# Routing tokens to experts: selection-matrix products on TensorE replaced by indirect DMAs through memory

## What is computed

```python
cap = max(1, int(T * CAP_FACTOR / E))          # 512 * 1.25 / 8 = 80
probs_full = jax.nn.softmax(xt @ gate_w, axis=-1)
top_p, top_i = lax.top_k(probs_full, K)        # K = 2 of E = 8
for k in range(K):
    e, w = top_i[:, k], top_p[:, k]
    pos = ...                                  # how many earlier tokens chose e in choice k
    keep = pos < cap
    buf = zeros((E, cap, D)).at[e, pos_c].set(xt * keep, mode='drop')
    h = gelu(einsum('ecd,edf->ecf', buf, w1) + b1)             # 512 -> 2048
    y = einsum('ecf,efd->ecd', h, w2) + b2                     # 2048 -> 512
    y = y + einsum('ecr,erd->ecd', gelu(einsum('ecd,edr->ecr', buf, wd)), wu)
    out = out + y[e, pos] * keep * w
sh = gelu(xt @ sw1 + sb1) @ sw2 + sb2 + gelu(xt @ swd) @ swu   # a shared expert for all tokens
out = out + 0.2 * sh
```

## Time and profile before

| | us |
|---|---|
| median of 3 runs (2127.96 to 2133.68) | 2129.24 |
| the profiled execution | 2133.98 |
| its span in the trace | 2132.3 |
| of it, from the first expert's first product to the last one's end | 1758.4 to 2117.3 |
| PE busy | 2012.3 (94%) |
| DVE / ACT / POOL busy | 1193.0 / 1038.2 / 292.6 |

### The profile page before, as it was taken

How to read it: one execution, slowest core, us unless ns; L and a number is a source line. 1 busy time by engine, 2 the same in 40 slices (tenths; PEclk the granted TensorE clock), 3 DMA queues, 4 the chain that set the end, 5 groups by cost and what they waited for, 6 DMA issues and landing times. The chain is left out here.

```text
span 2132.3 us, 33366 instructions
## 1 busy us (share of the span) xinstructions
PE 2012.3 (94%) x10596; PEld 1662.8 (78%) x10596; DVE 1193.0 (56%) x2660; ACT 1038.2 (49%) x2357; POOL 292.6 (14%) x234
## 2 busy tenths in 40 slices
PE   7899999999999999999999999998797999999998
PEld 6787777877877778777877887786653789999997
DVE  3456666667666655666766766665766430222113
ACT  3202766676676661066676676668254431111111
POOL 0200112211211122011211112122232000000000
PEclk9899999999999999999999999999899999999998
DMA  7452111111111245311111111113003325544440
GB/s 217 165 175 82 36 42 42 45 32 47 42 33 37 61 157 180 121 33 38 53 30 44 40 34 47 35 43 91 30 0 101 148 113 220 198 191 160 160 161 20
DMA packets 121890, 186.66 MB, mean 88 GB/s; under 512 B 11896, under 2 KB 69424, under 8 KB 117712
## 3 DMA queue, kind: packets, MB, share of 16 engines
q1 hardware_dynamic: 119136, 181.06, 25.4%
q10 hardware_dynamic: 2672, 4.55, 0.7%
HBM read 146.78 MB, written 38.80 MB: 87 GB/s over the span
## 5 line engine op out<-in xcount | busy, mean ns | idle before, releaser
L698 DVE TENSOR_TENSOR crs_ptl<-crs_tp,crs_pth 128x512 fp32r<-128x512 f32 x512 | 352.2, 690 | 226.7 <-ACT crs_pth L566 225.7
L566 ACT ACTIVATE crs_pth<-crs_tp 128x512 fp32r<-128x512 f32 x512 | 305.1, 596 | 209.8 <-PE crs_tp L910 209.8
L495 POOL TENSOR_TENSOR crs_vl<-crs_vraw,crs_vh 128x512 fp32r<-128x512 f32 x128 | 165.1, 1290 | 1117.3 <-ACT crs_vh L573 1117.3
L901 PE MATMUL crs_ring<-crs_kh,crs_ql 128*128 128x512 f32 x512 | 235.2, 459 | 3.9 <-DVE crs_ql L738 3.9
L920 PE MATMUL crs_ov<-crs_ptl,crs_vh 128*128 128x512 f32 x512 | 208.6, 407 | 19.0 <-DVE crs_ptl L698 19.0
L910 PE MATMUL crs_tp<-all_ident,crs_prob 128*128 128x128 f32 x1024 | 197.3, 274 | 26.7 <-ACT crs_more L560 26.7
L910 PEld LDWEIGHTS crs_tp<-all_ident,crs_prob 128*128 128x128 f32 x1024 | 138.6, 140 | 101.7 <-ACT crs_more L560 44.3
L901 PE MATMUL crs_ring<-crs_kh,crs_qh 128*128 128x512 f32 x512 | 202.8, 396 | 0.0
L920 PE MATMUL crs_ov<-crs_pth,crs_vh 128*128 128x512 f32 x512 | 202.3, 395 | 0.0
L901 PE MATMUL crs_ring<-crs_kl,crs_qh 128*128 128x512 f32 x512 | 201.8, 394 | 0.0
L920 PE MATMUL crs_ov<-crs_pth,crs_vl 128*128 128x512 f32 x512 | 200.2, 391 | 0.0
(11 more groups left out here) (264 smaller groups left out, 3594.2 us busy)
## 6 DMA issues: line engine op xcount, KB each, us to landing
moe_w<-in_L_ffn_w SPq DMA_DIRECT2D x48, 1024.0 KB, 11.6
v_scratch<-crs_more SPq DMA_DIRECT2D x64, 512.0 KB, 2.9
crs_vraw<-v_scratch SPq DMA_DIRECT2D x128, 256.0 KB, 2.7
ex_w<-in_L_ffn_w SPq DMA_DIRECT2D x16, 1024.0 KB, 12.0
crs_prob<-in_ctx SPq DMA_DIRECT2D x32, 256.0 KB, 3.9
crs_wo<-in_L_xattn_Wo SPq DMA_DIRECT2D x16, 512.0 KB, 4.1
moe_w<-in_L_ffn_sw SPq DMA_DIRECT2D x8, 1024.0 KB, 14.3
qry_wq<-in_L_xattn_Wq SPq DMA_DIRECT2D x16, 256.0 KB, 4.3
```

The source lines that it names most:

```text
L495: nc.gpsimd.tensor_tensor(vl[:, n % VR, :, :], vraw[:, :, :], vh[:, n % VR, :, :].bitcast(F32), ALU.subtract).then_inc(s["v_lo"], 1)
L566: act.activation(pth[:, k % PT, :], tp[k % PT][:, :], ACT.Copy).then_inc(s["pt_hi"], 1)
L698: v.tensor_tensor(ptl[:, k % PT, :], tp[k % PT][:, :], pth[:, k % PT, :].bitcast(F32), ALU.subtract).then_inc(s["pt_lo"], 1)
L901: m = pe.matmul(ring[at % RING][:, :], a[:, t // RT, rows], w[:, n % KR, :], start=i == 0, stop=i == 2)
```

## The change

Two buffers in the device memory are added: `buf_dram` (8 experts x 2 choices x 80 slots x 512 words) and `y_dram` (the same for seven experts).

**Tokens to experts.** At the start of `experts` POOL clears `xe`, and SP writes these zeros over `buf_dram` in four DMAs. DVE works out for each token and choice the row in `buf_dram` (`idx`; a token that has no place gets a row past the end). POOL then writes the token rows there with eight indirect DMAs of 128 rows (2 KB a row). For every expert SP loads its 160 rows into `xe` (`rows_load`), PE turns them with 16 transposes (`fetch`) and ACT puts them into `bufT`. `fetch(e + 1)` stands in each expert but the last between its two layers. `gather`, `sel`, `xh` and `xl` are gone.

**Outputs back.** The turned rows of experts 0 to 6 go as they are to `y_rows` (ACT, no split), and SP writes them to `y_dram` (`rows_store`). When expert 6's have landed, POOL fetches for every token and choice its row with eight indirect DMAs into `y_got` (in the buffer of expert 6's `w1`, cleared by POOL first), and DVE adds these 8 tiles to `X` (`residual_got`) during expert 7. Only expert 7 still goes through `comb` and `scatter`.

The core of the diff:

```diff
         def _(sp):
+            sp.wait_ge(s["consts"], 1)
+            for m in range(E // 2):
+                sp.dma_start(buf_dram[2 * m:2 * m + 2, :, :, :].rearrange("e k s d -> s (e k) d"), xe[:, :, :, :].rearrange("s q k d -> s (q k) d")).then_inc(s["zeroed"], 16)
             expert_loads(0, 0)
-            sp.wait_ge(s["x_hi"], 2)
+            sp.wait_ge(s["routed"], TT * K * 16)
+            rows_load(0, 0)
             sp.wait_ge(s["sh_ps"], FC)
             expert_loads2(0, 0)
+            sp.wait_ge(s["xe_ld"], 16)
+            rows_load(1, 1)
...
                     sp.wait_ge(s["y_ps"], e * 2 + 2)
                     expert_loads(e + 2, q)
                     expert_loads2(e + 2, q)
+                    rows_load(e + 2, q)
+                    rows_store(e, q)
+            rows_store(E - 2, 0)
...
         def _(pool):
+            nc.gpsimd.memset(xe[:, :, :, :], 0.0).then_inc(c, 1)
...
+            pool.wait_ge(s["zeroed"], E // 2 * 16)
+            pool.wait_ge(s["ids_ok"], K)
+            for i in range(TT):
+                for k in range(K):
+                    nc.gpsimd.indirect_dma_start(buf_dram[:, :, :, :].rearrange("e k s d -> (e k s) d"), bass.IndirectOffsetOnAxis(idx[:, i, k:k + 1], 0),
+                                                 xn[:, i, :], None, bounds_check=E * SL - 1, oob_is_err=False).then_inc(s["routed"], 16)
+            pool.wait_ge(s["y_ps"], (E - 2) * 2 + 2)
+            nc.gpsimd.memset(y_got, 0.0).then_inc(c, 1)
+            pool.wait_ge(s["y_st"], E * 16)
+            for i in range(TT):
+                for k in range(K):
+                    nc.gpsimd.indirect_dma_start(y_got[:, i, k, :], None, y_dram[:, :, :, :].rearrange("e k s d -> (e k s) d"),
+                                                 bass.IndirectOffsetOnAxis(idx[:, i, k:k + 1], 0), bounds_check=(E - 1) * SL - 1, oob_is_err=False).then_inc(s["routed"], 16)
...
         def _(v):
+            def residual_got():
+                v.wait_ge(s["routed"], 2 * TT * K * 16)
+                for k in range(K):
+                    for i in range(TT):
+                        v.scalar_tensor_tensor(X[:, i, :], y_got[:, i, k, :], topp[:, i, k:k + 1], X[:, i, :], ALU.mult, ALU.add).then_inc(s["chain"], 1)
...
+            biased(0)
+            with v.Fori(1, E - 1) as e:
                 biased(e)
+            residual_got()
+            combine(E - 1)
+            biased(E - 1)
             turned(E - 1)
-            residual(E - 1)
+            residual()
...
         def _(pe):
+            def fetch(e, j, early=False):
+                pe.wait_ge(s["xe_ld"], e * 16 + 16)
+                if not early:
+                    pe.wait_ge(s["yt_hi"], e * K - K)
+                for m in range(2):
+                    for c in range(2):
+                        for k in range(K):
+                            at = c * SL + k * CAP
+                            p = pe.transpose(t_ps[m][:, at:at + CAP], xe[:, j, k, (2 * m + c) * P:(2 * m + c + 1) * P], ident[0:CAP, 0:CAP])
+                    p.then_inc(s["g_ps"], 1)
...
                 for n in range(3):
                     layer1(5 + n)
-                    if not first:
-                        pe.wait_ge(s["r_ok"], e + 1)
-                        scatter(e - 1, before == 1, 2 * n, 2 * n + 2)
-                if pair is not None:
-                    gather(pair + 1)
+                if not last:
+                    fetch(e + 1, 1 - i, first)
```

More of the change, by code:

```diff
@@ L1352, in _, with experts @@
                 m.then_inc(s["out_ps"], 1)
-def experts(nc, a, out, X, ident):
+def experts(nc, a, out, buf_dram, y_dram, X, ident):
     E, K = 8, 2
@@ L1377, in experts @@
     LOWEST = -87.5
+    NOWHERE = 65536.0
     with ExitStack() as ctx:
@@ L1723, in hidden, with turned, expert @@
                 m.then_inc(s["h_ok"], 1)
-            def turned(e):
+            def turned(e, q):
+                act.wait_ge(s["y_st"], e * 16)
                 for k in range(K):
                     act.wait_ge(s["yt_ps"], e * K + (k + 1))
-                    act.activation(yh[:, k, :], t_ps[k][0:CAP, :], ACT.Copy).then_inc(s["yt_hi"], 1)
-            def expert(e, first, pair=None):
+                    act.activation(y_rows[:, q, k, :], t_ps[k][0:CAP, :], ACT.Copy).then_inc(s["yt_hi"], 1)
+            def expert(e, q, first=False, last=False):
                 for n in range(4):
@@ L1851, in turn, with scatter @@
                     m.then_inc(s["yt_ps"], 1)
-            def scatter(e, first, start, stop):
-                if start == 0:
-                    pe.wait_ge(s["comb_ok"], e + 1)
-                    pe.wait_ge(s["yt_lo"], e * K + K)
-                for n in range(start, stop):
+            def scatter():
+                pe.wait_ge(s["yt_lo"], 2 * K)
+                for n in range(K * TT):
                     k, i = n // TT, n % TT
-                    if not (first and n < 2):
-                        pe.wait_ge(s["c_ok"], e * (K * TT) + (n - 1))
+                    if n >= 2:
+                        pe.wait_ge(s["c_ok"], n - 1)
                     for part in (yl, yh):
@@ L1863, in scatter, with expert @@
                     m.then_inc(s["c_ps"], 1)
-            def expert(e, i, uses, before, pair=None):
-                first = before == 0
+            def expert(e, i, uses, first=False, last=False):
                 pe.wait_ge(w1_ld[i], uses * 64)
-                pe.wait_ge(s["g_ok"], uses * KC)
+                pe.wait_ge(s["g_ok"], e * 2 + 2)
                 def layer1(n):
@@ L1911, in expert @@
                         m.then_inc(s["y_ps"], 1)
-                    if c == 0 and not first:
-                        scatter(e - 1, before == 1, 6, K * TT)
-            pe.wait_ge(s["x_hi"], 2)
             pe.wait_ge(s["rows_ok"], K)
             pe.wait_ge(s["so_ok"], 2)
-            gather(0)
+            fetch(0, 0, True)
             pe.wait_ge(s["so_ok"], TT)
             pe.wait_ge(s["sh_ok"], FC)
-            expert(0, 0, 1, 0)
-            expert(1, 1, 1, 1, 0)
-            with pe.Fori(0, (E - 4) // 2) as m:
-                expert(m * 2 + 2, 0, m + 2, 2)
-                expert(m * 2 + 3, 1, m + 2, 2, m + 1)
-            expert(E - 2, 0, E // 2, 2)
-            expert(E - 1, 1, E // 2, 2)
+            expert(0, 0, 1, first=True)
+            expert(1, 1, 1)
+            with pe.Fori(1, (E - 2) // 2) as m:
+                expert(m * 2, 0, m + 1)
+                expert(m * 2 + 1, 1, m + 1)
+            expert(E - 2, 0, E // 2)
+            expert(E - 1, 1, E // 2, last=True)
             turn(E - 1)
-            scatter(E - 1, False, 0, K * TT)
+            scatter()
 def perceiver(nc, a, out):
@@ L1947, in perceiver @@
             selfattn(nc, a, X, ident, prob)
-        experts(nc, a, out, X, ident)
+        experts(nc, a, out, buf_dram, y_dram, X, ident)
 def kernel(**inputs):
```

114 lines of the change are left out of this document (48 added, 66 removed).

## The result

| | before | after |
|---|---|---|
| median (us) | 2131.46 (2127.96 to 2133.73, 4 runs) | 2146.43 (2143.38 to 2147.17, 4 runs) |
| the profiled execution / its span | 2133.98 / 2132.3 | 2143.38 / 2141.6 |

The account below looks back on a forecast made before the run. PE's own instructions were taken to bound the kernel. +17.1 (experts 1 to 6) + 0.9 - 3.1 - 3.5 = +11.4 us gave an expected median of 2140.6 us, own range 2131 to 2149, overall range 2122 to 2155.

Parts of the forecast that it names:

- The wait: Experts 1 to 6: PE stands still 5.7 us before the fetch, for rows queued behind 8.5 MB of weights.
- the landing: SP's queue: the rows are there 25.3 us after the expert's start; bounds on average 24.6 and 26.3.
- The fetch: PE, between an expert's two layers: sixteen transposes per fetch, taken as 1.75 us.
- The clock: PE after each wait: granted clock falls to 0.50, costing 1.7 us on average; bounds 0 and 2.3.
- The price per expert: Experts 1 to 6: 25.3 + 1.75 + 20.0 + 1.7 = 48.75 us each, +17.1 in all.
- The front: Before expert 0: the gather becomes 16 transposes, most at 1.2 GHz, and a wait for ACT's copy; -3.5 us.
- The tail: Expert 7: eight indirect fetches take about 7.8 us back to back, within 19.7 us of room; cost 0.
- the third rival: Expert 7: POOL's fetches come one after another and make DVE 5.9 us late; 2146.5 us, chance 0.15.
- Rival 1: Experts 1 to 6: rows land at 24.6 us and the clock holds; 2126.2 us, chance 0.17.
- Rival 2: Experts 1 to 6: no wait, rows do not stand behind the weights; -33.0 us, 2096.2 us, chance 0.08.
- Expert 0: Expert 0: no wait; PE's gap of 0.86 us before the second layer is filled by 1.75 of transposes; +0.9 us.
- Expert 7: Expert 7: loses 3.74 us of scatter and gets back 0.6 of the gap between its layers; -3.1 us.

Follow-up runs that it names:

- filled wait: Changed kernel with 24 more products, results unused, on PE between first layer and fetch in experts 1 to 6: 2135.67 us.
- both halves: Outputs back by indirect DMAs alone: 2109.69 us; routing by DMA alone, rows ahead of weights, against the kernel before: 2115.95 us.
- one moved line: Changed kernel with SP issuing the load of an expert's rows ahead of that expert's weights instead of behind them: 2096.35 us.

## Why the prediction was right

**The wait** (the main term) was right in its place and its cause: six waits ahead of the fetch of experts 2 to 7, 6.7 us each where 5.7 were predicted. The mis-sized term is the landing: PE's first transpose came 26.6 us after the expert's start on average in place of 25.3, outside the bounds of 24.6 to 26.3. (The terms written down for it, 23.7 + 0.8 + 0.6, give 25.1, not 25.3.) It was the weights ahead of the rows and not the rows. In the trace of the changed kernel the last 1 MB of `w2` landed 24.5 to 26.4 us after the expert's start, 25.7 on average (in the expert shown issued at 1849.99 and there 15.6 us later); in the kernel before, whose times I had carried over, 23.6 to 25.5, on average 24.5. The rows landed 0.8 behind the weights, and PE began 0.1 later. Why the weights came 1.2 us later in this trace than in that one is not shown. The 358 GB/s of the Trainium skill's page "DMA: Bandwidth & Descriptors" (Specifications), by which the wait would have been 7.9 us, do not explain it: the queue moved 383 to 391 GB/s in this trace in the eight us up to 1863, and what the wait had more than predicted came behind that.

**The fetch** was miscounted: eight transposes, not sixteen. The row of the turn, eight in 0.87 us, was read rightly and doubled wrongly. The fetch cost 0.6 us at full clock (1815.39 to 1816.00 above), not 1.75, and 1.1 at the half clock; half of the bound by the 80 columns, 0.55, comes near it.

**The clock** fell as predicted. I took 1.7 us with bounds up to 2.3. In the rows of the changed kernel it cost 2.2: 0.5 more in the fetch and 1.7 on average in the first group of the second layer (5.67 to 7.04 in place of 4.61). The filled wait measured 1.8 to 2.1.

**The price per expert** came out at 26.6 + 0.6 + 20.0 + 2.2 = 49.4 (49.46 measured) against the predicted 48.75: the landing 1.3 and the clock 0.5 too low, the fetch 1.15 too high. That these errors nearly cancel is luck. With eight transposes in 0.87 the six experts would have been predicted 5.3 us lower, and the front and expert 0 together some 2, so that by the same working the sum would have been near +4. The wait and the half clock are the right mechanism; that the number came so close is not their merit alone.

**The front** gave back 5.7 in place of 3.5: the fetch to expert 0's first product took 1.44 us. PE had not stopped ahead of it, so the transposes ran at full clock, and they are eight:

```profile
1746.23 0.77 PE L1883 MATMUL moe_bank<-all_ident,moe_xe 80*128 80x80 f32 x8
1746.76 0.77 ACT L1749 ACTIVATE moe_bufT<-moe_bank 128x320 f32<-128x320 f32 x2 [8.14 <-PE moe_bank L1883]
...
1747.67 2.74 PE L1914 MATMUL moe_bank<-moe_bufT,moe_w 128*128 128x160 f32 x9 [0.67 <-ACT moe_bufT L1749]
```

**The tail** is hidden, as forecast, and the third rival did not come. From the timeline of expert 7 of the changed kernel, which began at 2085.80 (L1545 the indirect fetches, L1660 `residual_got`, L1667 the bias of the expert's output):

```profile
2100.07 1.06 POOL L1545 DMA_INDIRECT moe_w<-y_scratch,moe_idx  x1 [10.62 <-DMA y_scratch<-ex_y_rows]
...
2109.28 1.00 POOL L1545 DMA_INDIRECT moe_w<-y_scratch,moe_idx  x1 [0.30 <-issue]
2112.70 5.51 DVE L1660 SCALAR_TENSOR_TENSOR all_X<-moe_w,moe_topp,all_X 128x512 f32<-128x512 f32 x8 [26.00 <-DMA moe_w<-y_scratch,moe_idx]
2118.25 0.88 DVE L1624 TENSOR_SCALAR ex_comb<-moe_rows,moe_ecol 80x512 fp32r<-80x512 f32 x2
...
2126.76 0.68 DVE L1667 TENSOR_SCALAR ex_yT<-moe_bank,moe_b_cols 128x160 f32<-128x160 f32 x2 [7.06 <-PE moe_bank L1938]
```

POOL fetches from 14.3 us into the expert (13.8 predicted), the eight take 12.6 us together (7.8 taken, bound 25.6), and DVE has 7.06 us to spare. The formula of the same page (Anatomy of one DMA) for one DMA from POOL, which the prediction put eight times in a row for an estimate of 20.8, is not what came: they go out 1.30 us apart, and the last is there 3.4 us after it began.

**Rival 1** (a cheaper wait) did not come: no rows landed before 25.5 us and the clock fell each time. **Rival 2** (no wait) was false for this kernel, and its price was near: 33.0 us less than before was worked out for rows that do not stand behind the weights, and with them ahead it is 35.8 (the experts take 40.85 us in place of 41.35, by the cheaper fetch).

**The rest.** Expert 0's +1.45 (0.9 predicted) is not the transposes, which only fill its gap of 0.86 in part. In the changed kernel the clock is 0.50 from about 1747.2 to 1750.7, at the start of expert 0, and its first 40 products take 12.56 us in place of 11.11: the half clock that stood in front of expert 0 before (1752 to 1755.2) has moved into it. So this term came near for another reason than the one given. Expert 7's -2.7 (-3.1 predicted) is the scatter's 3.74 less a gap of 0.92 before its second layer, which stays open.

## What to carry to other kernels

A small load that an engine waits for, issued behind megabytes on one queue, arrives when the megabytes have; issue it ahead of them or on another queue, and look at the whole queue before believing that traffic is free. A wait in an in-order engine costs what is queued behind it, and on PE the idle time is charged a second time by the clock (here 6.7 us of wait and about 2 of half clock). When a change loses, split it and move its new waits before giving it up: here both halves gain, and one moved line made +15 us into -36.

## What the runs showed that was not expected

- The clock also fell after short idle time: after 1.81 us in one expert, while it held after 2.24 in the one before.
- With sixteen indirect fetches of 128 rows in a row PE had 6.3 us of gaps, and ACT was held up too. With eight it was 0.8, and 0.8 to 0.9 with eight more plain loads of the same size, on SP's queue or POOL's. The cause is open.
- Eight float32 transposes that pass 80 columns took 0.6 us, where eight that pass 128 took 0.87.
